# Gate folded into the value weight, FFN normalisation on ScalarE, and the next batch's row work cut into single steps

## The reference, cut to what matters

```python
mod = (_silu(c) @ wmod).reshape(4, 6, 1, 256)          # sa, ca, ga, sb, cb, gb
ga = (2 * (ga >= 0) - 1) * jnp.maximum(jnp.abs(ga), 0.25)   # gb likewise
h  = _layernorm(x) * (1 + ca) + sa                     # x: 4 batches x 1024 rows x 256
x  = x + ga * attention(h)     # = h + softmax(causal(q k^T)) v o_proj, with a layernorm of h inside
h  = _layernorm(x) * (1 + cb) + sb
x  = x + gb * ffn(h)           # 704 wide, silu(gate) * up, router: top 2 of 8 rank-16 adapters
```

## Time and profile before

| | us |
|---|---|
| median of 3 runs | 710.68 (710.49 to 711.01) |
| the profiled execution | 710.4 |
| its span, first to last instruction | 708.6 |
| TensorE busy in the span | 665.5 (94%) |
| DVE busy | 509.1 (72%) |
| POOL busy | 392.2 (55%) |
| ACT busy | 340.2 (48%) |

### The profile page before, as it was taken

How to read it: one execution, slowest core, us unless ns; L and a number is a source line. 1 busy time by engine, 2 the same in 40 slices (tenths; PEclk the granted TensorE clock), 3 DMA queues, 4 the chain that set the end, 5 groups by cost and what they waited for, 6 DMA issues and landing times.

```text
span 708.6 us, 10697 instructions
## 1 busy us (share of the span) xinstructions
PE 665.5 (94%) x3760; PEld 561.0 (79%) x3760; DVE 509.1 (72%) x1152; ACT 340.2 (48%) x604; POOL 392.2 (55%) x518
## 2 busy tenths in 40 slices
PE   5879999999999999999999999999999999999995
PEld 3669977877789987877788897887778997788884
DVE  5996786688976778578986678677988669536323
ACT  4534354535355345454355436364445535454542
POOL 3794457537772257456774238554775245743644
PEclk9989999999999999999999999999999999999999
DMA  8400010000000010000000002000000000000000
GB/s 303 117 1 1 1 61 1 0 1 31 0 2 31 1 61 1 0 1 31 0 1 31 1 1 61 0 1 1 30 2 1 31 1 1 0 1 1 31 0 31
DMA packets 14037, 15.44 MB, mean 22 GB/s; under 512 B 1312, under 2 KB 12704, under 8 KB 13984
## 3 DMA queue, kind: packets, MB, share of 16 engines
q1 hardware_dynamic: 13984, 14.76, 6.4%
HBM read 10.57 MB, written 4.19 MB: 21 GB/s over the span
## 4 chain that ended last, share of the span: by engine, by line
PE 55%; DVE 28%; issue 9%; POOL 5%; ACT 2%; DMA 1%; POOLq 0%; SPq 0%; DVEq 0%; ACTq 0%
PE ps L1198 50%; PE ps L1207 5%; DVE hid L1068 4%; DVE zb L799 3%; DVE zb L817 3%; POOL ring_lo L441 2%; DVE zb L804 2%; DVE stat L814 1%; DVE tm_hi L1058 1%; DVE tm_lo L1058 1%; DVE xr L817 1%; DMA xs<-in_L_attn_x 1%; DVE onehot L1019 1%; DVE stat L951 1%; DVE mv L791 1%
## 5 line engine op out<-in xcount | busy, mean ns | idle before, releaser
L441 POOL TENSOR_TENSOR ring_lo<-hid,ring_hi 128x512 fp32r<-128x512 f32 x144 | 192.3, 1342 | 104.2 <-ACT ring_hi L684 103.4
L676 ACT ACTIVATE act_s<-ps 128x512 f32<-128x512 f32 x120 | 71.8, 599 | 150.3 <-PE ps L1198 150.3
L1068 DVE TENSOR_TENSOR hid<-act_s,ps 128x512 f32<-128x512 f32 x120 | 81.5, 681 | 78.7 <-ACT act_s L676 69.5
L684 ACT ACTIVATE ring_hi<-hid 128x512 fp32r<-128x512 f32 (+1 forms) x144 | 90.3, 627 | 18.9 <-DVE hid L1068 10.2
L429 POOL TENSOR_TENSOR xr<-xr,xs 128x256 f32<-128x256 f32 x32 | 23.4, 733 | 91.8 <-DVE xr L959 91.8
L1198 PE MATMUL ps<-wdT_hi,ring_hi 128*128 128x256 f32 x192 | 53.1, 282 | 0.0
L1198 PE MATMUL ps<-wdT_lo,ring_hi 128*128 128x256 f32 x192 | 52.5, 279 | 0.0
L1198 PE MATMUL ps<-xT_hi,wgT_hi 128*128 128x512 f32 x96 | 39.3, 409 | 8.1 <-DVE hid L1068 8.1
L631 ACT ACTIVATE pT_hi<-ps 128x512 fp32r<-128x512 f32 (+3 forms) x48 | 21.8, 488 | 47.8 <-PE ps L1207 47.5
L1198 PE MATMUL ps<-wdT_hi,ring_lo 128*128 128x256 f32 x160 | 44.6, 279 | 0.0
L1198 PE MATMUL ps<-tm_hi,bgT_hi 128*128 128x512 f32 x96 | 40.6, 423 | 3.4 <-DVE hid L1068 3.3
(11 more groups left out here) (219 smaller groups left out, 2074.6 us busy)
## 6 DMA issues: line engine op xcount, KB each, us to landing
xs<-in_L_attn_x SPq DMA_DIRECT2D x4, 1024.0 KB, 5.6
out<-xr SPq DMA_DIRECT2D x7, 512.0 KB, 2.9
s_mod<-in_L_wmod SPq DMA_DIRECT2D x1, 1024.0 KB, 8.8
s_qkvT<-in_L_attn_qkv SPq DMA_DIRECT2D x1, 768.0 KB, 10.5
s_wg<-in_L_ffn_Wg SPq DMA_DIRECT2D x1, 704.0 KB, 8.0
s_wu<-in_L_ffn_Wu SPq DMA_DIRECT2D x1, 704.0 KB, 9.4
s_wd<-in_L_ffn_Wd SPq DMA_DIRECT2D x1, 640.0 KB, 8.3
s_mod<-in_L_wmod SPq DMA_DIRECT2D x1, 512.0 KB, 6.8
```

The source lines that it names most:

```text
L441: pool.tensor_sub(ring[1][:, place(n), :], hid[:, n % HID, :], ring[0][:, place(n), :].bitcast(fp32)).then_inc(h_lo.sem, 1)
L676: nc.scalar.activation(act_s[:, n % 2, :], ps[:, 2 * (n % 2), :], ACT.Silu).then_inc(silu_ready.sem, 1)
L684: nc.scalar.activation(ring[0][p0:P, place(n), :], hid[p0:P, n % HID, :], ACT.Copy).then_inc(h_hi.sem, 1)
L1068: V.tensor_mul(hid[:, n % HID, :], act_s[:, n % 2, :], ps[:, 2 * (n % 2) + 1, :]).then_inc(h_ready.sem, 1)
```

## The change

1. **Gate in the value weight.** `wvo` is kept in fp32 (`wvo_full`). For each batch POOL multiplies it by the gate (`values_weight`), ACT writes the high part, POOL the low part. The residual becomes two POOL operations (`residual`: multiply, add). `x1_product` multiplies by `rinv` and adds `xs` in one DVE instruction, so POOL's `x1_row` goes. DVE no longer makes `gated`.
2. **FFN normalisation on ACT**: `Identity` with bias `-mean*rstd` (`shift`) and scale `rstd`. The guess has one more small DVE instruction, Newton one more POOL instruction. For LN2_B all three Newton iterations stand at r = 2 and the normalisation at r = 6 and 7 of chunk 0.
3. **TensorE's order in chunk 0**: the second transposes move from after the second base unit to before the third adapter unit; `logits(1)` moves one group later; the down products are spread anew (`FILL`), two being kept for group 2.
4. **The second router** goes to r = 12 (shift), 14, 15 and 16.
5. **Next batch's rows**: centre, scale, statistics in units of their own, in two groups LN1_HA (tiles 0 to 3) and LN1_HB (4 to 7). POOL: gated weight at r = 3 and 4, Newton of HA at r = 10, the residuals of tiles 0 and 1 at r = 15 and 16, Newton of HB at r = 16. The other six residuals go to the start of the next body. The normalised tiles go to other buffers (`z_tile`), and tiles 4 to 7 are normalised after chunk 1's last unit.

```diff
@@ POOL, before the loop and its body
-            def newton_step(lo, n, it, done):
+            def newton_step(lo, n, it, done, shifted=False):
...
+                elif shifted:
+                    link(last)
+                    pool.tensor_mul(shift[:, lo:lo + n], neg_mean[:, lo:lo + n], y).then_inc(done, 1)
...
             def residual(b, i):
-                pool.wait_ge(t_gated.sem, t_gated.at(b, i))
+                link(pool.tensor_mul(gated[:, i % 2, :], zb[:, i, :], bc[:, b, GA, :]))
                 pool.tensor_add(xs[:, i, :], xs[:, i, :], gated[:, i % 2, :]).then_inc(r_ready.sem, 1)
...
+            def values_weight(b):
+                pool.tensor_mul(gated[:, :, :], wvo_full[:, :, :], bc[:, b, GA, :].unsqueeze(1).to_broadcast([P, KT, D])).then_inc(wvo_scaled.sem, 1)
+            def values_weight_low(b):
+                pool.wait_ge(wvo_hi.sem, wvo_hi.at(b, 0))
+                pool.tensor_sub(wvo[1][:, :, :], gated[:, :, :], wvo[0][:, :, :].bitcast(fp32)).then_inc(wvo_lo.sem, 1)
...
+                for i in range(2, NT):
+                    residual(b, i)
...
                             if r == 2:
-                                newton(b, LN2_B, TC, TC, 0)
-                                newton(b, LN2_B, TC, TC, 1)
-                            if r == 3:
-                                newton(b, LN2_B, TC, TC, 2)
+                                for it in range(NEWTON):
+                                    newton(b, LN2_B, TC, TC, it)
...
                         elif not last:
-                            if 5 <= r < 5 + NT:
-                                residual(b + 1, r - 5)
-                            if r == 13:
-                                newton(b, LN1_H, 0, NT, 0)
-                                newton(b, LN1_H, 0, NT, 1)
+                            if r == 2:
+                                pool.wait_ge(gates_done.sem, gates_done.at(b + 1, 0))
+                            if r == 3:
+                                values_weight(b + 1)
+                            if r == 4:
+                                values_weight_low(b + 1)
+                            if r == 10:
+                                for it in range(NEWTON):
+                                    newton(b, LN1_HA, 0, TC, it)
+                            if r == 16:
+                                for it in range(NEWTON):
+                                    newton(b, LN1_HB, TC, TC, it)
                             if r == 14:
-                                newton(b, LN1_H, 0, NT, 2)
+                                pool.wait_ge(wvo_lo.sem, wvo_lo.at(b + 1, 0))
+                            if r in (15, 16):
+                                residual(b + 1, r - 15)
                         hid_low(b, ci * UPC + r)
@@ ACT
+            def normalise(i, dst, src, sig):
+                nc.scalar.activation(dst, src, ACT.Identity, bias=shift[:, i:i + 1], scale=rstd[:, i:i + 1]).then_inc(sig.sem, 1)
...
-                        if ci == 0 and r == 7:
+                        if ci == 0 and r in (6, 7):
+                            if r == 6:
+                                act.wait_ge(rstd_ready.sem, rstd_ready.at(b, LN2_B))
+                            for tile in range(TC + 2 * (r - 6), TC + 2 * (r - 5)):
+                                normalise(tile, zb[:, tile, :], xr[:, tile, :], z2_ready)
+                        if ci == 0 and r == 9:
                             for k in range(KT):
                                 tr_high(b, KT * NC + KT + k, xT[0][:, 2, k, :])
+                        if ci == 1 and not last:
+                            if r == 5:
+                                values_weight_high(b + 1)
@@ DVE
-                    V.scalar_tensor_tensor(xr[:, t, :], ps[:, 6 + t % 2, 0:D], rinv[:, t:t + 1], bc[:, b, GA, :],
-                                           ALU.mult, ALU.mult).then_inc(x1_scaled.sem, 1)
+                    V.scalar_tensor_tensor(xr[:, t, :], ps[:, 6 + t % 2, 0:D], rinv[:, t:t + 1], xs[:, t, :],
+                                           ALU.mult, ALU.add).then_inc(x1_ready.sem, 1)
...
-                        if 4 <= r < 4 + NT:
-                            ln1_h(b + 1, (r - 4,))
-                        if r == 4 + NT:
-                            moments(range(NT))
-                            guess(0, NT).then_inc(norm_ready.sem, 1)
+                        for i in {4: (0,), 5: (1,), 6: (2,), 7: (3,), 10: (4, 5), 12: (6, 7)}.get(r, ()):
+                            ln1_centre(b + 1, i)
+                        for i in {5: (0,), 6: (1,), 7: (2,), 8: (3,), 11: (4, 5), 13: (6, 7)}.get(r, ()):
+                            ln1_rows(b + 1, i)
+                        for i in {8: (0, 1, 2), 9: (3,), 12: (4, 5), 14: (6, 7)}.get(r, ()):
+                            ln1_stats(i)
+                        if r == 9:
+                            moments(range(TC))
+                            guess(0, TC).then_inc(norm_ready.sem, 1)
                         if r == 15:
-                            dve.wait_ge(rstd_ready.sem, rstd_ready.at(b, LN1_H))
-                        if r >= 15:
-                            for i in range(3 * (r - 15), min(3 * (r - 14), NT)):
-                                normalise(i, zb, z_ready)
+                            moments(range(TC, NT))
+                            guess(TC, TC).then_inc(norm_ready.sem, 1)
+                        if r == 13:
+                            dve.wait_ge(rstd_ready.sem, rstd_ready.at(b, LN1_HA))
+                        for i in {13: (0,), 14: (1,), 16: (2, 3)}.get(r, ()):
+                            normalise(i, zb, z_ready, z_tile(i))
+                if not last:
+                    dve.wait_ge(rstd_ready.sem, rstd_ready.at(b, LN1_HB))
+                    dve.wait_ge(stored, b * (16 * NC) + 32)
+                    for i in range(TC, NT):
+                        normalise(i, zb, z_ready, z_tile(i))
@@ PE
+                        pe.wait_ge(wvo_lo.sem, wvo_lo.at(b, 0))
...
-                FILL = (1, 2, 1, 1)
+                FILL = {(0, 0): (0, 0, 0, 0), (0, 1): (0, 1, 1, 1), (0, 2): (2, 2, 2, 1),
+                        (1, 0): (0, 0, 0, 0), (1, 1): (1, 2, 1, 1), (1, 2): (1, 2, 1, 1)}
```

More of the change, by code:

```diff
@@ L285, in pt_banks @@
             return [(first + q, q * TC, min(TC, i + 1 - q * TC)) for q in range(-(-(i + 1) // TC))]
-        LN2_A, LN2_B, LN1_X, LN1_H = range(4)
+        LN2_A, LN2_B, LN1_X, LN1_HA, LN1_HB = range(5)
         NEWTON = 3
@@ L552, in _ @@
             for i in range(TC, NT):
[L553 removed]
+                nc.scalar.activation(zb[:, i, :], xs[:, i, :], ACT.Identity, bias=neg_mean[:, i:i + 1]).then_inc(first_centred, 1)
             modulation(0, (0,))
@@ L607, in _ @@
             act.wait_ge(early_lo, EARLY)
-            queries_values(0, range(6))
+            queries_values(0, range(2))
+            values_weight_high(0)
+            queries_values(0, range(2, 6))
             def body(b, last):
@@ L641, in body @@
                         queries_values(b, (6 + i,))
+                    if i == NT - 2:
+                        act.wait_ge(rstd_ready.sem, rstd_ready.at(b, LN2_A))
+                        for tile in range(TC):
+                            normalise(tile, zb[:, tile, :], xr[:, tile, :], z2_ready)
                 tr_high(b, KT * NC, xT[0][:, 0, 0, :])
@@ L978, in body @@
                         mark(V.reciprocal(rinv[:, t:t + 1], rowsum[:, t:t + 1]))
-                        if i == NT - 1:
-                            dve.wait_ge(rstd_ready.sem, rstd_ready.at(b, LN2_A))
-                            for tile in range(TC):
-                                normalise(tile, xr, z2_ready)
                         for e, j0, nj in pt_banks(t):
@@ L1230, in _, with transposes, attention_transposes @@
                 last_mm.then_inc(product_ready, 1)
-            def transposes(b, q, bank, k, tiles, src=zb):
-                for t, i in enumerate(tiles):
-                    last = transpose(ps[:, bank, t * P:(t + 1) * P], src[:, i, k * P:(k + 1) * P], ident[:, :])
+            def transposes(b, q, bank, k, rows):
+                for t, row in enumerate(rows):
+                    last = transpose(ps[:, bank, t * P:(t + 1) * P], row[:, k * P:(k + 1) * P], ident[:, :])
                 last.then_inc(transposed.sem, 1)
-            def attention_transposes(b, n, src=zb):
+            def attention_transposes(b, n, rows):
                 for k in range(KT):
@@ L1240, in attention_transposes @@
                     pe.wait_ge(z_ready.sem, z_ready.at(b, (n + 1) * TC - 1))
-                    transposes(b, q, q, k, range(n * TC, (n + 1) * TC), src)
+                    transposes(b, q, q, k, rows)
             def queries(b, js=range(4)):
@@ L1268, in _ @@
             pe.wait_ge(consts_made, 6)
-            attention_transposes(0, 0, xr)
+            attention_transposes(0, 0, [xr[:, i, :] for i in range(TC)])
             for b in range(3, B):
@@ L1278, in _ @@
```

(26 more changed lines are left out.)

151 lines of the change are left out of this document (72 added, 79 removed).

## The result

The changed kernel takes 722.63 us in the median (722.21 to 723.98, 4 runs) against 710.68 (710.49 to 711.01, 4 runs): ratio 1.0169, 95% interval 1.0153 to 1.0186. It is slower, as forecast, but by 12 us where 4.3 were forecast (715.0), and lies 4.1 us above the upper end of the range (718.5). Its profiled execution took 722.21 us with a span of 720.4.

What follows compares the result with a forecast made beforehand. TensorE, busy 94%, was taken as the bound. Each of three batches +0.1 - 3.5 + 4.9 = +1.5, last batch -0.3, start +0.4: +4.6 on 710.4, so 715.0 us; own bounds 710.4 to 719.5, 8-in-10 range 705 to 718.5.

Steps and rivals of the forecast that it cites:

- Chunk 1, units 5 to 15: TensorE's three waits in chunk 1 all go, as DVE drops the gate product and whole-tile units: -3.5 us a batch.
- T: The end of unit 15 in chunk 1, from which later times are counted; 196.42 us in the kernel before.
- The roots at T + 9.0: POOL's Newton steps for tiles 4 to 7 of the next batch give `rstd` 9.0 us after unit 15 ends.
- The wait of "5 to 6 us" before the second group: TensorE waits this long on DVE before the second group of the next batch's transposes, in three batches.
- The table-load rival: `Identity` after the exponentials needs two table loads of 1.28 us per batch: 719 us; both slower rivals together 0.08.
- from T to the next queries: +4.9: End of chunk 1: late row work moves the queries from T + 11.8 to T + 16.7; bounds 4.0 and 5.5.
- Full blocking: DVE's four late normalisations go one per POOL operation, ending at T + 13.2, with queries at T + 17.3.
- The wait of 1.03 us before the transposes: Chunk 0, second transposes: ScalarE's normalisations and TensorE's new order remove this wait, -1.3 us.
- The new wait before unit 7: Chunk 0: three Newton iterations at r = 2 delay `hid_low(2)` and `hidden(5)`; wait 0.86, with refill +1.0 us.
- The router and gates: Chunk 0: picks and two gate steps before `hidden(17)` make TensorE wait, +0.4 us, between 0 and +1.
- Before the loop: +0.4 forecast: At the start, TensorE newly waits for the low part of the gated weight: +0.4 us, between -0.3 and +1.3.
- The rival "faster": Row work after unit 15 is in time and the 3.5 us stay: 700.3 us, half of it 705.3; chance 0.25.

Runs made afterwards that it cites:

- b1: The kernel before with 10 linked copies on VectorE in each of three batches, ahead of its last two normalisations of the next batch's rows; 733.74 us.
- e7: The changed kernel with the next batch's rows back in the old order, one group, and all residual rows at the attention's start; 701.05 us.
- e6: The changed kernel with residual rows 0 and 1 back at the attention's start, second group's mean, variance and Newton steps one unit earlier; 714.46 us.
- e8: The changed kernel with the second group's four normalisations on ScalarE instead of VectorE, and GpSimd computing the shifts; 713.50 us.

## Why the prediction was right and wrong

**The sign and the chain were right.** Chunk 1, units 5 to 15: -3.5 forecast, -3.54 measured (30.76 to 27.22 us from the sixth base unit to T). The roots at T + 9.0: T + 8.94. POOL done at T + 13.2: 206.46, T + 12.96. No wait of 0.2 us or more in the attention, as forecast. The wait of "5 to 6 us" before the second group came as 4.52, with 1.26 before the first group, which the prediction doesn't have; together 5.8. The table-load rival: ScalarE has 17 table loads before and 17 after. The Trainium skill, "ScalarE: Activation LUTs", section "Table sets: the hidden batching unit", says that identity is in every set; the trace agrees.

**The term that was mis-sized is "from T to the next queries: +4.9".** Forecast were queries at T + 16.7 instead of T + 11.8. Measured: T + 18.94 in the first batch, +7.1, and +7.7 and +7.9 in the next two. It has two parts.
- *The middle value.* Full blocking gave T + 17.3 (+5.5), and I took T + 16.7 in the hope that a normalisation slips into the gap between the residual's two instructions. DVE's four ended at T + 13.1, the end of full blocking. The second transposes so started at T + 13.25 instead of T + 12.5. That is 0.7 us a batch, 2.2 in all. The Trainium skill, "SBUF — State Buffer", section "Who interferes with whom", says that whoever issues first gets the shared pair of ports for the whole instruction; by my reading that would have given DVE the gap. The trace doesn't bear this reading out: POOL's second instruction followed 0.08 us behind the first, and DVE made one tile per POOL instruction.
- *The clock, missing altogether.* "TensorE needs 4.17 us" from the transposes to the queries was taken from a stream that had not stood still, and was then put behind a wait of five microseconds. It became 5.69, 6.24 and 6.47. That is 5.9 us in all, some three quarters of the miss of 7.6, and it took the term out of my bounds of 4.0 to 5.5.

The second part could have been read before. The kernel before has two long waits ahead of the loop, and behind both the same eight transposes last 1.94 us instead of 1.06 (b1, above, shows that such a wait doesn't always do this):

```profile
28.20 1.94 PE L1207 MATMUL ps<-ident,xr 128*128 128x128 f32 x8 [2.64 <-DVE xr L817]
39.96 1.94 PE L1207 MATMUL ps<-ident,xr 128*128 128x128 f32 x8 [3.98 <-DVE xr L817]
```

**Chunk 0.** The wait of 1.03 us before the transposes went, as forecast. The new wait before unit 7 came, 0.60 us against 0.86 (`hidden(5)` at 109.46, forecast 108.86, but TensorE reached it later as well). The router and gates: 0.28 on `hidden(17)`, 0.4 in the next two batches. Together -0.14 in the first batch, against +0.1.

**Before the loop: +0.4 forecast, +0.76 measured, for another reason.** The value weight's low part was in time. What came later by as much is the second group of the first batch's transposes (wait 4.83 us instead of 3.98).

**The sum.** Of the 11.8 us between the spans: forecast 4.6, and on top of it clock 5.9, blocking 2.2, start 0.4, chunk 0 and units 5 to 15 of chunk 1 -0.7 (three batches together), the last batch and the tail -0.5; together 11.9.

**Where I looked for the gain was half wrong.** I put the -3.5 us down to the dropped gate product "and no longer does a whole tile in one unit". e7 shows that the second half of that sentence was not needed for 3.3 of the 3.5 us. So gain and loss don't belong together: the gain stays with part 1 of the change, the loss goes with the two groups and the late residual rows. The rival "faster" named T + 7.3 as the point from which all is kept, 700.3 us; e7, which gets there by another way, has 701.05.

## What to carry to other kernels

A price read from a busy stream need not hold behind a wait: look in the trace for a matmul group that follows a wait of the length you forecast, and compare its duration. Where a step must come late, ask which of its engines is held off by a neighbour; the same four normalisations took 4.07 us on VectorE and 2.07 on ScalarE. And when a change has several parts, undo one at a time: here what e7 left in place carried 10 us of gain, and the new row order with two residual rows hid it behind 21.6 us of loss.

## What the runs showed of the hardware

- The granted clock fell to half behind TensorE's waits. By the length of the wait in the loop: at 4.2 to 5.65 us in nine batches of nine, at 2.72 to 3.6 in nine of nine, at 2.34 and 2.38 in three of six, at 0.65 to 0.7 in none of six. Where it fell behind a wait ahead of the second transposes, the work from there to the queries lost 1.3 to 2.8 us. Outside the loop it stayed full behind waits of 3.11 (b1) and 3.29 us (e6), and behind 2.96 us at the end of four kernels.
- In the changed kernel the clock fell although TensorE worked 2.5 us, on the first transposes and a down product, between a wait of 1.26 and one of 4.52.
- Filling this wait with matmuls that feed nothing made the kernel faster: 60 of them, 14 us of TensorE's time, gained 4.7 us.
- VectorE's normalisations beside GpSimd went at one per instruction of GpSimd: four took 4.07 us beside two of 0.72 and two of 1.29, while three took 2.08 us in e7 beside a single one of 1.29. A gap of 0.08 us between two GpSimd instructions gave VectorE no extra one. The same four on ScalarE took 2.07 us beside the same GpSimd instructions (e8).
